# An expert layer whose register-addressed tiles use each high half once, with a shorter routing and a deeper gather ring

## The reference, cut to what matters

```python
E, K = (12, 3); H, I = (256, 640)
probs = _softmax(einsum("bsh,he->bse", x, Wr) + br)
top_vals, top_idx = top_k(probs, K);  ew = softmax(top_vals)
for e in range(E):
    sel = top_idx == e                      # tokens that chose e
    w_e = sum(where(sel, ew, 0)) / maximum(sel.sum(), 1)   # one weight per expert
    h = relu(x @ w1[e] + b1[e]) @ w2[e] + b2[e]
    out = out + mask_e * (w_e * h)
phi = sigmoid(relu(out.mean(axis=1) @ Wp1 + bp1) @ Wp2 + bp2)   # one number per sequence
out = out * (1 - 0.8 * (phi > 0.7));  x = layernorm(x + out)
```

## Time and profile before

| what | us |
|---|---|
| median of three runs | 1383.55 |
| the profiled execution's own time | 1388.23 |
| span of its instructions | 1386.4 |
| attention, up to the last transposes of its output | about 1105 |
| routing, from the last logits to the first gather (1121.0 to 1147.8) | 26.8 |
| tiles 0 to 12 (1147.8 to 1233.5) | 85.6 |
| tiles 13 to 34 (1233.5 to 1354.4) | 121.0 |
| the end | 32.0 |

### The profile page before, as it was taken

One profiled execution on the slowest core, in us unless ns is written; L12 is line 12 of the kernel. 1 busy time (PEld: TensorE's weight loads), 2 busy tenths in 40 slices (PEclk: granted clock), 3 DMA queues, 4 the chain that ended last, 5 costly groups with the idle time before them and its releaser, 6 DMA issues.

```text
span 1386.4 us, 36342 instructions
## 1 busy us (share of the span) xinstructions
PE 1238.6 (89%) x13701; PEld 1042.9 (75%) x13701; DVE 1115.3 (80%) x2046; ACT 957.3 (69%) x2057; POOL 669.9 (48%) x578
## 2 busy tenths in 40 slices
PE   6689999999999999999999999999998624778893
PEld 3458898888888797988888888978797524666663
DVE  5678999999999999999999999999984777633334
ACT  4867878788788878787888878888874446422331
POOL 0534555455545545554645454554533254544541
PEclk8899999999999999999999999999999956989996
DMA  6000202020202111010203021110203391465443
GB/s 191 4 15 2 47 25 54 11 62 2 62 15 49 29 36 39 25 40 25 63 2 62 10 55 24 40 41 24 40 9 115 80 368 38 74 103 70 75 72 99
DMA packets 124872, 76.17 MB, mean 55 GB/s; under 512 B 93225, under 2 KB 117301, under 8 KB 123169
## 3 DMA queue, kind: packets, MB, share of 16 engines
q1 hardware_dynamic: 115648, 51.84, 15.8%
q0 software_dynamic: 7760, 10.23, 5.0%
q10 hardware_dynamic: 1296, 11.80, 2.1%
HBM read 42.38 MB, written 10.09 MB: 38 GB/s over the span
## 4 chain that ended last, share of the span: by engine, by line
PE 74%; DVE 9%; issue 6%; DMA 5%; POOL 3%; ACT 2%; SPq 0%; POOLq 0%; ACTq 0%; DVEq 0%
PE bank L552 12%; PE bank L707 6%; PE bank L753 6%; PE bank L694 6%; PE bank L724 4%; PE bank L742 4%; PE bank L733 3%; PE bank L642 3%; PE bank L650 3%; PE bank L634 3%; PE bank L1632 2%; PE bank L602 2%; PE bank L603 2%; DVE con L1048 2%; PE bank L561 2%
## 5 line engine op out<-in xcount | busy, mean ns | idle before, releaser
L1048 DVE SCALAR_TENSOR_TENSOR con<-bank,taps,con 128x1022 f32<-128x1022 f32 (+2 forms) x192 | 245.3, 1277 | 22.6 <-ACT con L822 18.0
L552 PE MATMUL bank<-x,qkv 128*128 128x512 f16 x768 | 185.1, 393 | 6.9 <-DVE con L1048 6.9
L1205 POOL TENSOR_TENSOR gl<-const_sb,gc 128x512 f16<-128x512 f32 x128 | 129.8, 1039 | 120.2 <-DVE gc L1058 75.7
L552 PEld LDWEIGHTS bank<-x,qkv 128*128 128x128 f16 x768 | 73.7, 101 | 89.4 <-issue 9.6
L1240 POOL TENSOR_TENSOR oo<-oo 128x512 f16<-128x512 f32 x64 | 74.2, 1168 | 122.1 <-ACT oo L952 122.1
L1106 DVE TENSOR_TENSOR X<-X,bank 128x512 f16<-128x512 f16 x160 | 108.7, 680 | 17.2 <-PE bank L642 15.8
L1632 PE MATMUL bank<-xT,wts 128*128 128x128 f16 x1050 | 89.6, 238 | 31.5 <-DMA xT<-xg 25.8
L891 ACT ACTIVATE Z<-bank 128x512 f16<-128x512 f32 x160 | 96.3, 603 | 23.7 <-PE bank L650 23.7
L1097 DVE TENSOR_TENSOR Y<-bank,ymask 128x512 f16<-128x512 f32 x160 | 109.1, 683 | 2.9 <-PE bank L634 2.3
L1632 PEld LDWEIGHTS bank<-xT,wts 128*128 (+1 forms) x1050 | 74.7, 105 | 48.1 <-issue 39.2
L753 PE MATMUL bank<-out,sqo 128*128 128x256 f16 x768 | 98.3, 280 | 13.8 <-DMA sqo<-oo 8.1
(11 more groups left out here) (274 smaller groups left out, 3897.7 us busy)
## 6 DMA issues: line engine op xcount, KB each, us to landing
wts<-in_w ACTq DMA_DIRECT2D x7, 1280.0 KB, 12.5
w_qkv<-in_W_qkvz SPq DMA_DIRECT2D x16, 512.0 KB, 4.2
w_out<-in_W_out SPq DMA_DIRECT2D x16, 256.0 KB, 3.0
w_z<-in_W_qkvz SPq DMA_DIRECT2D x16, 256.0 KB, 2.7
wts<-in_w SPq DMA_DIRECT2D x2, 1280.0 KB, 7.1
spare_w<-in_w ACTq DMA_DIRECT2D x2, 1280.0 KB, 14.8
sum_rows<-zero SPq DMA_DIRECT2D x2, 1152.0 KB, 10.7
room<-in_w SPq DMA_DIRECT2D x1, 1280.0 KB, 22.0
```

The source lines that it names most:

```text
L552: last = mm(bank[:, b], qkv16[:, w, a, t * P:(t + 1) * P], x16[:, x, a, b * S:(b + 1) * S], start=(a == k == 0), stop=(a == HT - 1 and k = ...
L1048: stt(out=out, in0=bank[:, 0:B, 0:S - k], scalar=taps[:, par, t, TAPS - 1 - k:TAPS - k], in1=out, op0=ALU.mult, op1=ALU.add).then_inc(tap_ ...
L1205: last = tt(gl[:, g % 2, k].rearrange("p (m r) d -> p m r d", m=2), upper.unsqueeze(1).unsqueeze(1).broadcast_to([P, 2, R, P]), gc[:, par, ...
```

## The change

Line numbers in this section are those of the changed kernel where a row of it is shown.

1. **Tiles 12 to 34.** Each high half of w1 is loaded once and multiplied by both halves of x side by side (256 columns), the low half of w1 by x's high half (128 columns): 20 products. In `second` the high half of h is multiplied by both halves of w2 side by side (512 columns, so w2's halves are now stored beside each other), its low half by w2's high half: 10 products. The two column groups are added outside TensorE: for the hidden layer VectorE adds the second group (read from PSUM, three banks a tile instead of two) to what ScalarE wrote, and applies relu afterwards; for the output VectorE sums pairs. Tiles 0 to 11 keep their products. The expert's weight is applied in ScalarE's first step, for all tiles.
2. **Low halves.** All 24 of the weights and the 4 of y are made on VectorE; GpSimd makes none, and the scaled copies on ScalarE are gone.
3. **Routing.** The top three are taken from the logits, the softmax and the weights of the tokens are worked out behind the gathers' list, slots are formed by fewer products, the one-hot matrices by 48 small operations on float16 (with the token number in the same operation) instead of 4 wide ones and one on GpSimd. VectorE no longer waits for all small parameters at this point.
4. **Rings.** 8 buffers `xT` instead of 4, `xg` stays at 4; GpSimd gathers 8 tiles ahead.
5. **Loads.** Experts 2 to 4 are loaded on ScalarE's queue before the last transposes of the attention, 5 to 11 on SP's queue.
6. **Biases.** They stay in SBUF and are added in `join`; the products for them stand at tiles 9 to 12.
7. **Zero fill.** It moves from the first head to the ninth, right behind the load of W_out.

```diff
         def load_rest(n, par, which):
             if n or which != "qkv":
                 load(n, par, which)
+            if n == NK // 2 and which == "out":
+                clear()
...
-                experts.load_rest(sp)
-        run(sp, {"load": load_rest, "oT": tail}, then={("load", "out"): clear})
+                experts.load_late(sp)
...
                 experts.load_next(act)
...
             do(oo16[:, g, 0], oo[:, 4 * g:4 * g + 4], ACT.Copy).then_inc(oo_high, 1)
+            if n == NK - 1 and g == 1:
+                experts.high(act, 1, 0)
             if n == NK - 1 and g == 3:
-                act.wait_ge(oT_in[3], 16 * NK)
-                experts.load_late(act)
+                experts.high(act, 1, 1)
+                experts.high(act, 2, 0)
...
+            if n == NK - 1 and g == 3:
+                experts.low(dve, 1, 0)
...
-XB, OB = 4, 4
...
+GB, XB, OB = 4, 8, 4
...
+WIDE_BANKS = (0, 3)
...
-LOW_POOL = [(2, 0), (2, 1), (3, 0), (3, 1), (4, 0), (4, 1)]
...
-    def load_rest(sp):
-        sp.dma_start(index[:], ins["index"]).then_inc(par_in, 16)
-        sp.dma_start(before[:], ins["before"].partition_broadcast(P)).then_inc(par_in, 16)
+        sp.dma_start(index[:], ins["index"]).then_inc(wr_in, 16)
+        sp.dma_start(before[:], ins["before"].partition_broadcast(P)).then_inc(wr_in, 16)
...
     def load_next(act):
-        load_expert(act, 2)
-    def load_late(act):
-        for e in range(3, 6):
+        for e in range(2, 5):
             load_expert(act, e)
+    def load_late(sp):
+        for e in range(5, 7):
+            load_expert(sp, e)
...
-            low_done(act, e - 3, 1)
...
-        if (e, w) in LOW_POOL:
-            nc.scalar.activation(src, src, ACT.Copy, scale=SCALE).then_inc(w_scaled, 1)
...
+            for k in range(4):
+                dve.wait_ge(y16_high, k + 1)
+                nc.vector.tensor_tensor(y16[:, 2 * k:2 * k + 2, H:2 * H], y[:, 2 * k:2 * k + 2],
+                                        y16[:, 2 * k:2 * k + 2, 0:H], ALU.subtract).then_inc(y16_low, 1)
...
+        for e in range(7, E - 2):
+            load_expert(sp, e)
+        sp.wait_ge(y16_out, 64)
+        load_expert(sp, E - 2)
         sp.wait_ge(logits_full, 4)
         load_expert(sp, E - 1)
         for j in range(SPARSE):
-            sp.wait_ge(gathered[j % XB], 16 * (j // XB) + 16)
+            sp.wait_ge(gathered[j % GB], 16 * (j // GB) + 16)
             if j >= XB:
                 sp.wait_ge(h_full, 2 * (j - XB + 1))
-            sp.dma_start_transpose(out=xT[:, j % XB], in_=xg[:, j % XB]).then_inc(turned[j % XB], 16)
-            if j == E:
-                low_done(sp, E - 2, 1)
+            sp.dma_start_transpose(out=xT[:, j % XB], in_=xg[:, j % GB]).then_inc(turned[j % XB], 16)
+            if j == E + 3:
+                low_done(sp, E - 3, 1)
...
         def first(j):
             if j < E:
                 low_done(pe, j, 0)
             if j == E:
                 pe.wait_ge(tile_known, 1)
+                pe.wait_ge(b1_ready, 1)
+            if j == E + 1:
+                pe.wait_ge(b_evac, 4)
...
             pe.wait_ge(turned[j % XB], 16 * (j // XB) + 16)
+            if j == E:
+                pe.wait_ge(h_evac, 2 * E)
+            x = xT[:, j % XB].rearrange("p (x a) t -> p a x t", x=2)
             for half, ts in enumerate((PARTS_A, PARTS_B)):
                 if j >= 2:
-                    pe.wait_ge(h_evac, 2 * (j - 2) + half + 1)
-                out = bank[:, H_BANKS[j % 2][half]]
+                    pe.wait_ge(h_evac if j < E + 2 else h_sum, 2 * (j - 2) + half + 1 - (0 if j < E + 2 else 2 * E))
                 for i, t in enumerate(ts):
                     for a in range(HT):
-                        for k, (w, x) in enumerate(PARTS):
...
+                        at = slice(a * I + t * P, a * I + (t + 1) * P)
+                        if j < E:
+                            for k, (w, part) in enumerate(PARTS):
+                                last = mm(bank[:, H_BANKS[j % 2][half], i * P:(i + 1) * P], weights(j, 0, w, at), x[:, a, part],
+                                          start=(a == k == 0), stop=(a == HT - 1 and k == len(PARTS) - 1))
+                            continue
+                        both = bank[:, WIDE_BANKS[j % 2] + t // 2, 2 * P * (t % 2):2 * P * (t % 2 + 1)]
+                        mm(both, weights(j, 0, 0, at), x[:, a], start=(a == 0), stop=False)
+                        last = mm(both[:, 0:P], weights(j, 0, 1, at), x[:, a, 0], start=False, stop=(a == HT - 1))
                 last.then_inc(h_full, 1)
         def second(j):
...
                 if t in (0, PARTS_B[0]):
                     pe.wait_ge(h_low, 2 * j + (1 if t == 0 else 2))
...
+                at = slice(2 * t * H, 2 * (t + 1) * H)
+                hi, lo = (h16[:, j % 2, k, t * P:(t + 1) * P] for k in range(2))
+                if j < E:
+                    mm(out[:, 0:H], hi, rows2[:, j, 1, at.start:at.start + H], start=(t == 0), stop=False)
...
+                mm(out, hi, both_rows(j, at), start=(t == 0), stop=False)
+                last = mm(out[:, 0:H], lo, both_rows(j, slice(at.start, at.start + H)), start=False, stop=(t == IT - 1))
...
+        extras = {5: spread_biases, 7: lambda: turn_gates(0), 8: lambda: turn_gates(1),
+                  **{9 + k: (lambda k=k: biases(k)) for k in range(4)}}
...
-        weights = iter([(1, 0), (1, 1), (2, 0), (2, 1)])
+        weights = iter([(2, 1), (3, 0), (3, 1)])
         for g in range(4):
...
-            load_expert(act, 6 + g)
             if g < 3:
                 high(act, *next(weights))
-        high(act, *next(weights))
-        act.wait_ge(chance, 1)
+        act.wait_ge(chance, 2)
         do(prob[:], prob[:], ACT.Exp).then_inc(chance, 1)
-        load_expert(act, E - 2)
-        high(act, 3, 0)
+        do(ew[:], ew[:], ACT.Exp).then_inc(chance, 1)
+        act.wait_ge(par_in, 96)
...
         act.wait_ge(weight, 1)
-        do(ew[:], ew[:], ACT.Exp).then_inc(weight, 1)
-        high(act, 3, 1)
-        do(b2_16[:, 0], b2[:], ACT.Copy, scale=SCALE).then_inc(b2_parts, 1)
...
+        do(ew[:], best[:, :, 0:TOPK], ACT.Exp).then_inc(weight, 1)
+        high(act, 4, 0)
+        high(act, 4, 1)
+        high(act, 5, 0)
...
                 if j == 0 and half == 0:
                     act.wait_ge(ids_full, 1)
+                    act.wait_ge(share_made, 2)
                 if j >= 2:
                     act.wait_ge(h_low, 2 * (j - 2) + half + 1)
...
                 for i, t in enumerate(ts):
...
+                    if j < E:
+                        src, kind, bias = bank[:, H_BANKS[j % 2][half], i * P:(i + 1) * P], ACT.Relu, b1s[:, j, t:t + 1]
+                    else:
+                        src = bank[:, WIDE_BANKS[j % 2] + t // 2, 2 * P * (t % 2):2 * P * (t % 2) + P]
+                        kind, bias = ACT.Identity, b1d[:, t, j - E:j - E + 1]
+                    last = do(h32[:, j % 2, t * P:(t + 1) * P], src, kind, bias=bias, scale=gsh[:, j:j + 1])
...
+            if j + 5 < E:
+                high(act, j + 5, 1)
+            if j + 6 < E:
+                high(act, j + 6, 0)
...
-        dve.wait_ge(wr_in, 32)
-        dve.wait_ge(par_in, 128)
-        low(dve, 1, 0)
+        copy(iota16[:], index[:, IOTA]).then_inc(consts_made, 1)
         dve.wait_ge(logits_full, 4)
...
-        tt(hi_hot, index[:, IOTA][:, 0:SPARSE].unsqueeze(1).broadcast_to(wide),
...
+            for m in range(M):
+                last = ts(hi_hot[:, k * M + m], iota16[:, 0:SPARSE], tile_k[:, k, m:m + 1], index[:, TOKEN][:, m:m + 1],
+                          ALU.is_equal, ALU.mult)
...
+                last = ts(low_hot[:, k * M + m], iota16[:], low_k[:, k, m:m + 1], None, ALU.is_equal)
...
+        dve.wait_ge(chance, 4)
...
+        low(dve, 1, 1)
...
+        low(dve, 2, 0)
...
+                b = WIDE_BANKS[j % 2]
+                rest = bank[:, b:b + 3].rearrange("p b c -> p (b c)").rearrange("p (t x c) -> p t x c", x=2, c=P)
+                stt(out=h.rearrange("p (t c) -> p t c", c=P), in0=rest[:, c // P:d // P, 1], scalar=gsh[:, j:j + 1],
+                    in1=h.rearrange("p (t c) -> p t c", c=P), op0=ALU.mult, op1=ALU.add).then_inc(h_sum, 1)
+            for half, (c, d) in enumerate(((0, 2 * P), (2 * P, I))):
+                h = h32[:, j % 2, c:d]
+                if j >= E:
+                    dve.wait_ge(h_sum, 2 * (j - E) + half + 1)
+                    ts(h16[:, j % 2, 0, c:d], h, 0.0, None, ALU.max).then_inc(h_high, 1)
...
+                    stt(out=h16[:, j % 2, 1, c:d], in0=h, scalar=0.0, in1=h16[:, j % 2, 0, c:d], op0=ALU.max, op1=ALU.subtract)\
...
-            ts(osb[:, j % OB], bank[:, O_BANKS[j % 2], 0:H], gsh[:, j:j + 1], None, ALU.mult).then_inc(o_evac, 1)
...
-        for x in todo[0:4]:
+                dve.wait_ge(added[j % 2], 16 * ((j - OB) // 2 + 1))
...
+                copy(osb[:, j % OB], out[:, 0:H]).then_inc(o_evac, 1)
+            else:
```

(19 more changed lines are left out.)

285 lines of the change are left out of this document (132 added, 153 removed).

## The result

Four runs of the changed kernel gave 1346.2 us in the median (1344.3 to 1349.2), four of the kernel before 1383.3. The ratio is 0.974, 95% interval 0.971 to 0.976. The prediction was 1332.5, with a range of 1319 to 1350. The profiled execution took 1347.3 us (span 1345.5): 40.9 us less than the profiled one of before, where the sum said 51.0.

A forecast was written before the change was run, and what follows sets the result against it. TensorE bounds the attention loop, its queue and ring waits tiles 13 to 34, VectorE the routing. Terms -25.7 - 12.3 - 16.4 + 2.5 + 0.9 = -51.0 us against the median 1383.55 gave 1332.5, range 1319 to 1350.

The forecast's parts named there:

- since the profiler runs beside: Conversion to the median of 1383.55: it lies 4.7 below the profiled 1388.2 because the profiler runs beside that execution.
- Tiles 13 to 34: TensorE's queue sets the tile time; fewer register instructions take it from 4.79 to 4.2 us; 95.3 against 121.0, -25.7.
- the first rival: Tiles 13 to 34: queue doesn't run ahead of the wide products, a tile stays at 4.8; +12.6, 1345; chance 0.14.
- a `first` clearly shorter than 2.8: Sign in tiles 13 to 34: if seen, the forecast is wrong, the queue's price not being per register instruction.
- some 12 us of waits for the ring: Tiles 13 to 34: part of the 25.7 us gain, gone since gathers run 8 tiles ahead without the bias DMA.
- Tiles 0 to 12: First gather to tile 13: VectorE bounds, first(13) waits 4.0 us for bias rows; 69.2 against 85.6, -16.4.
- The zero fill: Ninth head: fill holds the queue until 614.9 at the latest, 3.8 us after the transposes' turn; +2.5 (0 to +5).
- The early loads: Attention's end: ScalarE issues two more loads, +0.8; last transposes delayed by loads in flight, +2.0 (0 to +3.9).
- The chain of norm and ScalarE: Before the logits: ScalarE makes weight halves while idle, GpSimd no longer waits behind it; -3.0 us (0 to -5).
- The one-hot matrices: Routing: 48 operations, bounds 0.07 and 0.20 us each, 3.4 to 9.6; 5.5 taken against 5.8, -0.3.
- The rest of the routing: Wait for small parameters and a low half gone, -5.2; `pick` without GpSimd beside it, -2.2; softmax steps moved or gone, -4.4.
- The second rival: Tiles 0 to 12: the first tiles wait for the expert loads; some +7, 1339.5; chance 0.17.

The follow-up runs named there:

- experiment 6: Changed kernel with the narrow products of before in tiles 12 to 34 and none of VectorE's additions of column groups: 1358.5 us.
- experiment 7: Changed kernel with fixed weight addresses from tile 12 on, no register instructions or loads of the expert number (result not the reference's): 1326.6 us.
- Experiment 5: Changed kernel with 4 turned tiles in the ring instead of 8: 1384.2 us.
- experiment 1: Changed kernel with the zero fill back in the first head: 1338.7 us.
- experiment 2: Changed kernel with experts 3 and 4 loaded on SP's queue behind the attention's last transposes, only expert 2 ahead on ScalarE's: 1344.3 us.
- experiment 3: Changed kernel with the 24 one-hot operations of 35 columns replaced by two wide operations: 1344.9 us.
- experiment 9: Also written e8_all: changed kernel with fill in first head, experts 3 and 4 loaded later, wide one-hot operations, fourth bias group at tile 11: 1332.5 us.
- experiment 11: One small plain DMA added on GpSimd's queue to the kernel of experiment 9 with experts 10 and 11 loaded behind transposes of tiles 3 and 5: 1328.1 us.
- experiment 12: Token product moved to GpSimd in the kernel of experiment 9 with experts 10 and 11 loaded behind transposes of tiles 3 and 5: 1329.9 us.
- experiment 8: Kernel before the change with a ring of 7 turned tiles instead of 4: 1365.8 us.

## Why the prediction was right, and where it was 13.7 us off

**The number.** 1346.2 lies inside the stated range, but above the 1323 to 1342 that the forecast gave as its own. Of the 13.7 us, 10.1 are terms of the sum, and 3.6 come from the step that took the profiled execution of before to lie 4.7 us above its median "since the profiler runs beside" it. The profiled execution of the changed kernel is 1.1 us above its median, those of the twelve variants between 1.9 below and 1.0 above theirs. So no other run shows such a price of the profiler; the 4.7 is more likely the scatter of one execution (the kernel before ran between 1377.8 and 1390.4 us in this study), and the column "before" of the table contains it; which stretches hold it is not shown.

**Tiles 13 to 34: right, and for the reason given.** The step "30 register instructions and 0.62" for 4.79 and "25 x 0.139 + 0.62 = 4.10" for the wide form gave 4.2 a tile, and 4.15 was measured. The two parts were less exact than their sum: a register instruction costs 0.124 and the rest of a tile 1.05 (experiments 6 and 7), and the two errors nearly cancel. The queue does run ahead, so the first rival falls; its 1345 is near the measured time by the accident of other losses. I had written that a `first` clearly shorter than 2.8 would speak against a price per register instruction. It is 2.5, and that sentence was wrong, as this row of half the register instructions of `first` shows, those ahead of the wide products (ns, first and last start):

```profile
L1656 PEldq FUSED_REGOPS  x230: 46/46/46, 1207.7 to 1305.0; - x115
```

The first of them starts at 1207.7, the first product that needs it at 1208.69. Some of the 20 are done while TensorE still computes something else, so the price shows in the period and not in `first` alone. In tile 21 it is seen too: the first products start at 1249.16 and after at the pace of their columns, and only from 1249.74 on at that of the queue.

What the prediction treated as two separate amounts (some 12 us of waits for the ring, the rest for the queue) is an order. Tiles 13 to 34 in four combinations:

| | narrow products | wide products |
|---|---|---|
| ring of 4 | 121.0 | 121.3 |
| ring of 7 or 8 | 108.2 and 108.0 | 94.4 |

With the ring of 4 the loop scatter, gather, transpose gives 5.5 us a tile, whatever the products cost. The wide products alone would have brought nothing.

**Tiles 0 to 12: right** (68.6 for 69.2), with VectorE busy for 90% of it and the wait at first(13) 2.65 us where the step said 4.0. Experiment 5 adds what the step did not have: a ring of 4 would have cost 8.7 us of it.

**The zero fill: mechanism right, size wrong.** The step was "the queue is free at 614.9 at the latest, 3.8 us after the transposes' turn; +2.5". It cost 7.0 (7.4 by experiment 1). Two terms were missing: the 2.8 us from issue to the first packet, and the lower clock after the stall, 5.91 - 3.06 = 2.85 us from the first group to the product behind the second. With the wait of 4.45 that makes 7.3.

**The early loads: undersized.** "+0.8" for ScalarE's issuing and "0 to +3.9, I take half, +2.0" for the transposes were 4.7 together by experiment 2. The waits for the transposes grew by 11.3 - 7.4 = 3.9, the upper end of the term, and the wait for ScalarE by 1.0. The chain of norm and ScalarE, "-3.0", was about as thought: with only expert 2 ahead, 34.6 us became 31.3, -3.3.

**The one-hot matrices: wrong.** "bounds 0.07 and 0.20 us each; I take 5.5" was 8.8. Both forms cost near the upper end (0.20 and 0.17), so the 35 columns saved nothing against 128. Since the two differ in their steps too, no run shows how much of it is a fixed part. The rest of the routing came out as reckoned: -9.2 - 3.0 = -12.2, where the sum had -5.2 - 2.2 - 4.4 = -11.8.

**The end: +2.5 that no row pointed to**, GpSimd's last instruction.

The second rival (first tiles wait for the loads) did not occur in the changed kernel, but by luck. The rate of the DMA engines there (40 slices of 1.125 us from 1115 on):

```profile
GB/s 168 247 137 428 437 437 419 391 18 206 343 285 259 400 428 401 417 428 410 437 428 428 437 428 410 428 182 27 0 0 117 11 219 119 149 200 26 205 119 195
```

It falls off at about 1145, 2 us ahead of the first gather (1147.12) and 5 ahead of the first transpose (1150.15). Part of that lead is owed to the terms that came out too long: the early loads and the one-hot matrices held up the list of tokens. Each edit that made the list earlier ran into the loads (experiments 2, 3, 9). The Trainium skill, "DMA: Bandwidth & Descriptors", section on queues, rings and completion order, has it that the transposes stand behind the loads of their own ring. By that order alone the whole delay would sit at the transposes; the trace of `e8_all` agrees in part only, since 3.4 of its 4.8 us lie in the gather, which has another queue.

Summed up, the miss is 4.5 (fill) + 1.7 (before the logits) + 2.9 (routing, one-hot) - 0.7 - 0.8 (tiles) + 2.5 (end) = 10.1 us, and 3.6 for the median of before make 13.7.

## What to carry to other kernels

When two limits lie close together, name the one that ends last and ask what each part is worth alone: here the wide products gained 13.6 us behind a deeper ring, and nothing in front of it. A transfer moved out of a quiet start into a loop without slack costs what the loop's own transfers come late by (4.45 us here), and the lower clock after the stall nearly two thirds of that again (2.85). Loads can be early or late; each place where something small must pass (a transpose, a gather) wants them out of the way, and the best version here put two of them behind the first tiles.

## What was not expected of the hardware

- A register instruction between TensorE's products costs 0.124 us of queue time, whatever the number of products around it. Products with fixed addresses go back to back: 3.28 us for 7680 columns, one column per 0.427 ns.
- VectorE's operations with a scalar per partition: 0.20 us for 35 columns with two steps, 0.17 us for 128 columns with one (starts 0.166 us apart). Two wide operations of 840 values take 2.07 us where 24 small ones took 4.89.
- VectorE's 24 float16 operations grew by 1.40 us beside 1.60 us of GpSimd's work. GpSimd's same product took 2.51 us beside VectorE's wide float32 comparisons before the change.
- GpSimd's last instruction takes 4.22 and 4.34 us in the two kernels of the old form and 6.62 to 6.71 us in the changed kernel and its eleven variants. A plain DMA, vector work on GpSimd and the depth of the ring do not explain it (experiments 11, 12, and 5 with 8); the cause stays open, 2.4 us.
